# Scores of a three-bank half's last unit placed behind the value products of tile 47

## The reference

```python
q = (query @ Wq + bq).reshape(B, Nq, H, D).transpose(0, 2, 1, 3)
k = (key @ Wk + bk).reshape(B, Nk, H, D).transpose(0, 2, 1, 3)
v = (value @ Wv + bv).reshape(B, Nk, H, D).transpose(0, 2, 1, 3)
attn = jax.nn.softmax(jnp.einsum('bhqd,bhkd->bhqk', q, k) * SCALE, axis=-1)
out = jnp.einsum('bhqk,bhkd->bhqd', attn, v)
```

## Time and profile before

| | |
|---|---|
| runs | 3850.76, 3851.41, 3845.80 us |
| median | 3850.76 us |
| the profiled execution | 3845.02 us |
| its span | 3843.3 us |
| granted clock, mean | 0.983 |
| busy: TensorE, ScalarE, VectorE, GpSimd | 96%, 66%, 47%, 13% |
| halves 2 to 5 of attention 2 | 2726.9 to 3096 us of the span |

### The profile page before, as it was taken

One profiled execution on the slowest core, in us unless ns is written; L12 is line 12 of the kernel. 1 busy time (PEld: TensorE's weight loads), 2 busy tenths in 40 slices (PEclk: granted clock), 3 DMA queues, 4 the chain that ended last, 5 costly groups with the idle time before them and its releaser, 6 DMA issues.

```text
span 3843.3 us, 84313 instructions
## 1 busy us (share of the span) xinstructions
PE 3675.9 (96%) x32244; PEld 1395.2 (36%) x32248; DVE 1791.7 (47%) x1805; ACT 2539.4 (66%) x2568; POOL 504.1 (13%) x1853
## 2 busy tenths in 40 slices
PE   7999999999999999999999999999999999897989
PEld 4333333335433333333333333342222223453444
DVE  3222222224277777777777777743211111343344
ACT  5999999992455555555555555479999999301321
POOL 1222222220000000000000000023322232001210
PEclk8999999999999999999999999999999999998999
DMA  5323232211111111111111110000000000000000
GB/s 185 97 75 107 81 101 84 97 71 62 57 38 41 37 40 39 42 40 38 39 38 39 38 43 1 1 23 4 4 4 4 4 30 2 18 27 0 0 13 28
DMA packets 104955, 162.83 MB, mean 42 GB/s; under 512 B 23108, under 2 KB 46048, under 8 KB 103104
## 3 DMA queue, kind: packets, MB, share of 16 engines
q1 hardware_dynamic: 104640, 158.16, 12.8%
HBM read 93.24 MB, written 64.88 MB: 41 GB/s over the span
## 4 chain that ended last, share of the span: by engine, by line
PE 76%; ACT 12%; issue 6%; DVE 4%; DMA 0%; ACTq 0%; SPq 0%; POOL 0%; DVEq 0%; POOLq 0%
PE ps L978 18%; PE ps L1003 18%; PE ps L667 10%; ACT probs L1347 7%; ACT probs L1358 4%; PE ps L599 4%; PE ps L489 3%; PE ps L495 3%; PE ps L882 3%; PE ps L861 2%; PE ps L1154 2%; PE ps L1165 2%; PE ps L1213 2%; PE ps L1227 1%; PE ps L868 1%
## 5 line engine op out<-in xcount | busy, mean ns | idle before, releaser
L1475 ACT ACTIVATE probs<-ps 128x1024 f32<-128x1024 f32 x808 | 828.4, 1025 | 588.4 <-PE ps L978 576.2
L1358 ACT ACTIVATE probs<-ps 128x1024 f32<-128x1024 f32 x1200 | 1119.6, 1031 | 50.3 <-PE ps L599 41.7
L2319 DVE TENSOR_TENSOR vbuf<-vbuf,probs 128x1024 f32<-128x1024 f32 x784 | 953.2, 1223 | 331.7 <-ACT probs L1475 331.7
L667 PE MATMUL ps<-probs,vst 128*32 128x512 f32 x6400 | 844.6, 599 | 27.0 <-ACT probs L1358 24.1
L2131 DVE COPY qs<-ps 128x512 f32<-128x512 f32 (+1 forms) x208 | 141.7, 681 | 570.4 <-PE ps L495 282.2
L1347 ACT ACTIVATE probs<-ps 128x1536 f32<-128x1536 f32 x268 | 362.1, 1604 | 8.2 <-PE ps L667 5.7
L1638 POOL CAST kst<-kb 128x128 fp32r<-128x128 f32 (+1 forms) x800 | 252.8, 316 | 751.3 <-PE ps L667 577.4
L978 PE MATMUL ps<-probs,kb 64*64 64x512 f32 x2560 | 332.2, 589 | 0.0
L978 PE MATMUL ps<-probs,qz 64*64 64x512 f32 x2048 | 268.3, 594 | 3.1 <-DVE cols L1843 2.8
L1003 PE MATMUL ps<-probs,qz 64*64 64x512 f32 x2048 | 267.2, 592 | 1.8 <-DVE kb L2344 1.8
L1003 PE MATMUL ps<-probs,kb 64*64 64x512 f32 x2048 | 265.8, 589 | 0.0
(11 more groups left out here) (433 smaller groups left out, 3626.3 us busy)
## 6 DMA issues: line engine op xcount, KB each, us to landing
kv_scratch<-qs SPq DMA_DIRECT2D x192, 256.0 KB, 2.0
kb<-kv_scratch SPq DMA_DIRECT2D x72, 256.0 KB, 2.8
qz<-kv_scratch SPq DMA_DIRECT2D x64, 256.0 KB, 2.9
kb<-k_scratch SPq DMA_DIRECT2D x12, 816.0 KB, 6.9
vbuf<-in_L_ffn_W SPq DMA_DIRECT2D x32, 256.0 KB, 3.1
klo<-kv_scratch SPq DMA_DIRECT2D x32, 256.0 KB, 2.9
k_scratch<-klo SPq DMA_DIRECT2D x12, 512.0 KB, 4.7
qs<-kv_scratch SPq DMA_DIRECT2D x24, 256.0 KB, 2.9
```

The source lines that it names most:

```text
L667: mm = pe.matmul(ps[band, 6 + half, :], vst[:, r, band], probs[:, r, j * HT:(j + 1) * HT], start=start, stop=stop)
L1358: act.activation(probs[:, r, b * T:(b + 1) * T].rearrange("p (h n) -> p h n", h=2), ps[:, 2 * buf:2 * buf + 2, :], ACT.Exp, scale=HD8 ** - ...
L1475: act.activation(pr1[:, (u + (u == LAST1) + 2 * odd) % 4], ps[:, 2 * b:2 * b + 2, :], ACT.Exp, scale=HD64 ** -0.5)\
L2319: dve.tensor_tensor(sum1[:, odd, h], sum1[:, odd, h], e, ALU.add).then_inc(s["added"], 1)
```

## The change

Unit 66 of a half by triples was issued in turn 15, ahead of the value products of tile 47. It is now issued at the top of turn 16, behind them. All else keeps its order: GpSimd still stages keys ahead of values.

```diff
                 def by_triples(gh):
                     for i in range(ST // RING):
                         last = i + 1 == ST // RING
-                        if not last and (i or gh - 1 not in TRIPLES):
+                        if i or gh - 1 not in TRIPLES:
                             qk_triple(gh, 4 * i + 2)
                         ring_jobs(gh, i)
                         if last:
@@ -806,8 +806,6 @@
                             begin2(gh + 1, 2)
                         else:
                             qk_triple(gh, 4 * i + 5)
-                        if i + 2 == ST // RING:
-                            qk_triple(gh, LAST3)
                         values2(gh, 3 * i + 2)
```

## The result

| | before | after |
|---|---|---|
| median of 14 runs | 3850.61 us | 3841.49 us |
| lowest to highest | 3841.4 to 3855.39 | 3838.15 to 3846.07 |
| profiled execution: time, span | 3845.02, 3843.3 us | 3840.84, 3839.1 us |

The ratio is 0.9981, with a 95% interval from 0.9974 to 0.9988: 7.3 us less, 4.6 to 10. (The two medians alone lie 9.1 us apart, the two means 7.9; the text goes by the ratio with its interval.) The forecast was 5.1 us less and 3844.4 us.

A forecast was written before the change was run, and what follows sets the result against it. ScalarE's exponentials were taken to pace attention 2's halves 2 to 5. Three ends at 1.3 us plus 1.2 at half 5 gave 5.1 us (range 4 to 6.5), hence 3844.4 us (range 3838 to 3849.6).

The forecast's parts named there:

- What bounds the stage: Attention 2, halves 2 to 5: ScalarE sets the pace, busy 362.1 of 369 us; only its 8.2 us idle can be gained.
- Tile 47 at 0.43 us behind unit 65, unit 66 1.00 us behind it: TensorE at the end of half 4: tile 47 at 3000.19, unit 66 free to start at 3001.19.
- the edit's own price: Ends of halves 2 to 5: unit 66 starts 0.26 us later, since tile 47 doesn't fit whole under exp 64.
- Weight loads: Unit 66's loads behind tile 47, taken as nothing; rival with them bare: 2.8 us gained in all, 3846.7 us, chance 0.14.
- Exp 66, unit 0, exp 0 to 2: End of half 4: exp 66 gains 0.73 us, unit 0 stops waiting for keys, exp 0 gains 1.36, exp 2 1.33.
- End of half 5: Next half goes by pairs; first full group of four at about 3099.1 instead of 3100.29, a gain of 1.2 us.
- Nothing given back later: After exp 2 engines stand to each other as before, so the rest of the half keeps 1.3 us.
- From the sum to the time: Whole kernel: 5.1 us off the median gives 3845.7, off the mean of four 3843.1; half way, 3844.4 us.
- the lower centre: Starting time for the forecast, between the median of three timed runs and the mean of four (3848.2 us).
- "nothing": Rival: waits at exp 0 to 2 fill up again, or the edit does nothing; 3849.5 us, chance 0.09.
- the slower rival: Granted clock falls at the four ends, value products take 1.94 us instead of 1.06; 9.3 us slower, 3857.5, chance 0.03.

The follow-up runs named there:

- the run with keys first on the changed kernel: GpSimd stages the next half's first keys ahead of tile 50's values, against the changed kernel; exp 65 to exp 2 took 6.58, 6.57 and 6.57 us.
- the same on the kernel before: GpSimd stages the next half's first keys ahead of tile 50's values, against the kernel before; exp 65 to exp 2 took 7.13 us at three ends.
- the runs with cut sums: Changed kernel with the previous half's sums (L713) cut into column pieces; ratio to the kernel before 0.9976 with two pieces, 0.9970 with four.
- the three later comparisons: Changed kernel with the previous half's sums behind tile 4, in two pieces, or in four; ratios to the kernel before 0.998, 0.9976 and 0.9970.
- the split run: Two heads of tile 47's products ahead of unit 66, two behind, against the changed kernel; exp 65 to exp 2 took 8.12, 8.14 and 8.12 us.

## Why the prediction was right or wrong, point by point

- **What bounds the stage**: right. ScalarE's busy time didn't change, its idle time did.
- **Tile 47 at 0.43 us behind unit 65, unit 66 1.00 us behind it**: 2996.43, 2996.86, 2997.86. Right to a hundredth, and so the edit's own price, 0.26 us, as worked out.
- **Weight loads**: priced at nothing; right. Weight loads of the end of half 4, after:

```profile
2997.86 0.18 PEld L647 LDWEIGHTS ps<-qz,kst 32*128 32x128 f32 x2 [0.84 <-issue]
2998.28 0.19 PEld L647 LDWEIGHTS ps<-qz,kst 128*128 128x128 f32 x1 [0.24 <-issue]
```

  Unit 66 took 0.92 us from its first matmul, against 0.94 before, and started no later behind tile 47 than unit 65 behind tile 46. If the rule of the Trainium skill that was weighed there ("TensorE: Matmul & The Clock Gate", Part 3) decided here, three loads of 0.19 us would have made it 0.57 us later; this trace shows no such cost.
- **Exp 66, unit 0, exp 0 to 2**: the table above; every step within 0.02 us. That keys would stop being late rested on working alone; the rows of GpSimd above and the run with keys first on the changed kernel show it, and the same on the kernel before gives them a price that the prediction had not set apart, 0.79 us of an end.
- **End of half 5**: 1.2 us forecast, 7.55 less 6.34 is 1.21.
- **Nothing given back later**: right within attention 2. The one gap that remains in each half, before exp 6, I had not counted; it is in both kernels and cost the forecast nothing.
- **From the sum to the time**: here the forecast was off by 2.9 us, inside its range. I set the centre between the median of three runs and the mean of four, as if two kinds of run were alike in number. The 14 runs put the median of before at 3850.61, where the first median was: ten lie from 3849.82 to 3855.39 and four from 3841.4 to 3847.37. From the median alone the forecast would have been 3845.7 us, 4.2 off; that the lower centre came nearer was luck, since it made up for a timed gain that was under-forecast. That gain, 7.3 us, lies above my own range of 4 to 6.5 and above the 5.24 that the traces show in the stage, though its interval, 4.6 to 10, holds the 5.24 and the 5.1 forecast. In the profiled pair the rest goes both ways: 0.65 us were gained ahead of half 2 and 1.7 lost behind half 5. The stretches at half clock fall elsewhere there, with about the same sum (135 and 134 us); that they are the cause is not shown. Much of the scatter goes with the granted clock: of the 17 executions of the kernel before that stand beside the runs with cut sums, the eight with a mean clock of 0.981 took 3850.1 us on average, the six with 0.983 took 3844.4. In the three later comparisons the timed gain, by the ratio, is also above what the traces show in attention 2: 7.7, 9.2 and 11.5 us for 4.8, 7.7 and 7.7, each time within its interval. Whether some 2 us of the timed gain are more than scatter stays open; no row shows a cause.
- **Slips among the rivals**: the 3849.5 us of "nothing" is the forecast's centre plus 5.1, not "3848.2 less the rounding", and it stands for no gain, not for half of it; the slower rival counted from 3848.2 where the others counted from 3849.5, so that its 3857.5 should have been 3858.8. And the 1.78 us of idle time that it cites stood 1.6 us ahead of the product of 1.94 us, in front of the scores before it. None of this moved the forecast.
- **The slower rival** (granted clock): no stretch of attention 2's halves 2 to 5 was below 1.00 in either trace. It did not happen.

## What to carry to other kernels

Where an engine waits for another ahead of an instruction, look behind it for work that doesn't need that wait, and count who hangs on that work: here three readers did, and the end of the products mattered, not the filled wait (the split run filled it and lost). Work inserted between units that are only two ahead of the bounding engine is free up to a small size, here 0.26 us ahead of unit 6; moving it two tiles on gained nothing, and cutting it so that less stands ahead of one unit gained 1.3 us in the stage. And read a change of 0.2% by the starts of single instructions in its stage, where two executions agree to hundredths, not by one execution's total.

## What the runs showed of the hardware that I had not expected

- The value products of two heads take as long as those of four: 1.05 us for four recorded matmuls, 1.06 for eight. The first records of the four heads, each with its own 32 columns of the array, start 7 ns apart and last 0.62 us each, and the second records follow 0.45 us later; so the heads run beside each other, and splitting a tile by heads costs twice. Splitting by columns of the moving operand doesn't: the sums delay what follows by 0.85 us whole and by 0.42 a half (from start to the next unit's start: 0.97, 0.54, and 0.33 for a quarter).
- Exponentials of 1536 columns that follow without a gap start 1.33 to 1.34 us apart, one alone lasts 1.45 from start to end, and in a queue they are recorded with 1.7. A loop through both engines at the ends of halves pays the 1.45, 0.14 to the matmul, and 0.07 to 0.12 back.
